# Value product of attention: one block of four units per batch in place of two blocks of two

## The reference

```
q = rope(proj(layernorm(x), Wq, bq)) * Dh ** -0.5      # 16 heads of 16
k = rope(proj(ctx, Wk, bk));  v = proj(ctx, Wv, bv)
scores = einsum('bhqd,bhkd->bhqk', q, k)               # causal mask
probs  = softmax(scores)
out    = einsum('bhqk,bhkd->bhqd', probs, v)           # the value product
x      = x + tanh(g) * (out @ Wo.T + bo)
...                                                    # router, top 2 of 32 experts, capacity 140 per expert
```

## Time and profile before

| | us |
|---|---|
| median of 3 runs | 768.54 |
| lowest and highest run | 766.45, 773.82 |
| span of the profiled execution | 763.2 |
| TensorE (PE) busy | 669.2 (88%) |
| VectorE (DVE) busy | 525.3 (69%) |
| ScalarE (ACT) busy | 403.5 (53%) |
| GpSimd (POOL) busy | 323.1 (42%) |
| value product L1665 busy | 62.0 |

### The profile page before, as it was taken

The page is one execution under the profiler, slowest core; times in us unless marked ns, Lnnn a source line. Parts: engine busy times, 40 slices in busy tenths (PEclk is TensorE's granted clock), DMA queues, the critical chain, the costliest instruction groups (busy, mean ns, idle before and its releaser), DMA issues.

```text
span 763.2 us, 17579 instructions
## 1 busy us (share of the span) xinstructions
PE 669.2 (88%) x5275; PEld 530.8 (70%) x5275; DVE 525.3 (69%) x1548; ACT 403.5 (53%) x1569; POOL 323.1 (42%) x340
## 2 busy tenths in 40 slices
PE   8799999999999999999987313699999999999992
PEld 4466666666666666666655201499999999999992
DVE  6665786767867678676899888677778644445441
ACT  2367778877788777888684566022222222222220
POOL 3443362443624436243112000435566565665643
PEclk9899999999999999999999655799999999999996
DMA  5600010210102001010001601168888998888921
GB/s 182 221 32 25 26 51 24 74 27 25 50 23 73 26 25 50 23 49 1 26 26 49 242 0 16 44 195 229 263 259 249 266 269 255 269 235 267 276 42 15
DMA packets 57852, 85.83 MB, mean 112 GB/s; under 512 B 11452, under 2 KB 28468, under 8 KB 57652
## 3 DMA queue, kind: packets, MB, share of 16 engines
q1 hardware_dynamic: 47588, 74.37, 29.7%
q0 software_dynamic: 9216, 9.76, 7.8%
q10 hardware_dynamic: 976, 0.89, 0.4%
HBM read 72.30 MB, written 12.69 MB: 111 GB/s over the span
## 4 chain that ended last, share of the span: by engine, by line
PE 49%; ACT 19%; DVE 18%; issue 8%; DMA 2%; POOL 2%; ACTq 1%; DVEq 1%; POOLq 0%
PE pair L1005 19%; PE bank L1015 10%; ACT arena L1311 8%; DVE arena L1484 5%; PE pair L1637 4%; PE bank L1600 3%; ACT arena L574 2%; PE pair L1646 2%; PE bank L1665 2%; ACT arena L1260 2%; PE bank L1027 2%; PE pair L1632 2%; ACT arena L1299 1%; DMA arena<-rows,slot_row 1%; DVE we L1465 1%
## 5 line engine op out<-in xcount | busy, mean ns | idle before, releaser
L1311 ACT ACTIVATE arena<-pair,arena 112x112 f32<-112x112 f32 x512 | 175.5, 365 | 67.0 <-DVE arena L1484 62.2
L1005 PE MATMUL pair<-arena,we 128*128 128x140 f32 x1024 | 137.9, 283 | 0.7 <-issue 0.6
L896 POOL DMA_INDIRECT rows_out<-arena,slot_row x64 | 94.4, 1475 | 94.6 <-DVE arena L949 81.4
L1005 PEld LDWEIGHTS pair<-arena,we 128*128 128x128 f32 x1024 | 128.5, 190 | 1.2 <-issue 1.2
L926 ACT ACTIVATE arena<-pair 128x140 f32<-128x140 f32 x160 | 45.8, 287 | 149.6 <-PE pair L1005 103.0
L961 DVE SCALAR_TENSOR_TENSOR arena<-arena,pair 128x140 f32<-128x140 f32 x160 | 47.6, 297 | 95.5 <-ACT arena L926 50.4
L1311 ACT ACTIVATION_READ_ACCUMULATOR arena<-pair,arena 112x1 f32 x512 | 109.8, 214 | 0.0
L885 POOL DMA_INDIRECT arena<-rows,slot_row x64 | 63.1, 986 | 83.8 <-issue 83.8
L1015 PE MATMUL bank<-arena,we 128*128 128x140 f32 x512 | 83.7, 286 | 0.0
L1484 DVE TENSOR_REDUCE arena<-pair 112x8 f32<-112x896 f32 x64 | 68.9, 1077 | 17.4 <-PE pair L1637 16.8
L1646 PEld LDWEIGHTS pair<-tab,arena 112*112 112x112 f32 x512 | 51.5, 133 | 30.3 <-issue 28.3
(11 more groups left out here) (209 smaller groups left out, 1195.2 us busy)
## 6 DMA issues: line engine op xcount, KB each, us to landing
we<-w_experts_in SPq DMA_DIRECT2D x192, 256.0 KB
wa<-w_adapters_in SPq DMA_DIRECT2D x16, 384.0 KB
arena<-ctx_in SPq DMA_DIRECT2D x8, 448.0 KB, 4.4
arena<-x_in SPq DMA_DIRECT2D x8, 448.0 KB, 4.0
rows_out<-arena SPq DMA_DIRECT2D x8, 448.0 KB, 3.3
rows<-arena SPq DMA_DIRECT2D x8, 448.0 KB, 3.3
arena<-ways_in SPq DMA_DIRECT2D x1, 1024.0 KB, 5.2
arena<-rows,slot_row POOLq DMA_INDIRECT x64
```

Source lines behind the costliest of these rows:

```text
L896: nc.gpsimd.indirect_dma_start(d["out"], bass.IndirectOffsetOnAxis(ap=slot_row[:, h, e:e + 1], axis=0), yr[e % 2][:, h, :], None, compute_ ...
L1005: last = nc.tensor.matmul(banks[m % 4][:, part * CAP:(part + 1) * CAP], w[:, col0:col0 + 128], xet[j % 2][:, c, :], start=(c == 0), stop=( ...
L1311: last = nc.scalar.activation(pr[s % 2][:, j, :], banks[BS[s % 4]][0:T, j * T:(j + 1) * T], ACT.Exp, bias=nmx[s // 2 % 2][:, s % 2, j:j + ...
```

## The change

The value product of a batch is issued in one call. `WEIGH` goes from 5 to 7 and the call is made for every fourth unit, at steps 7, 11, 15 and 3. It loops over the four units inside the loop over heads, so that four matmuls in a row go to the four column tiles. It waits for the evictions of all four units, and counts one per batch on `s_pv` in place of two. The turned probabilities of two batches are kept: `prt` has eight buffers, four of them in the arena as before, four in the part of `we[1][1]` behind `pcos`. The waits on `s_pv` of the evictions and of the value and attention reads are put in the new count.

```diff
-TURN, WEIGH, DENOM, SUMS, ATT = 2, 5, 6, 7, 8
+TURN, WEIGH, DENOM, SUMS, ATT = 2, 7, 6, 7, 8
+KEPT_UNITS = 2 * NU
...
-    prt = [take(T, [HU, T]) for _ in range(4)]
...
+    prt_at = [2 * NT + i * HU * T for i in range(NU)]
+    prt = [we[1][1][0:T, at:at + HU * T].rearrange("p (a b) -> p a b", a=HU) for at in prt_at]
+    prt += [take(T, [HU, T]) for _ in range(NU)]
...
                     if u % 2 == 1:
                         wait(act, s_ptr, GU * (g - back) + u + 1)
-                        wait(act, s_pv, GU // 2 * (g - back) + u // 2 - 1)
-                        nc.scalar.copy(prt[u % 4].rearrange("p a b -> p (a b)"),
+                        wait(act, s_pv, GB * (g - back) + u // NU - 1)
+                        nc.scalar.copy(prt[u % KEPT_UNITS].rearrange("p a b -> p (a b)"),
... (the same on VectorE for even units)
-            wait(dve, s_pv, GU // 2 * (q - 1))
+            wait(dve, s_pv, GB * (q - 1))
...
-                        wait(dve, s_pv, GU // 2 * (g - back) + (u + NU) // 2)
+                        wait(dve, s_pv, GB * (g - back) + u // NU + 1)
...
-        def weigh(q, par, u):
-            b, k = u // NU, u % NU
-            if u == 0:
+        def weigh(q, par, b):
+            if b == 0:
                 wait(pe, s_v, 2 * (q + 1))
-            if k == 0:
-                wait(pe, s_att, GB * q + b)
+            wait(pe, s_att, GB * q + b)
             for i in range(2):
-                wait(pe, s_pte[i], GU // 2 * q + u // 2 + 1)
+                wait(pe, s_pte[i], GU // 2 * q + NU // 2 * (b + 1))
             for j in range(HU):
-                for i in range(2):
-                    h = head_of(k + i, j)
-                    rows = slice(32 * (k + i), 32 * (k + i) + 32)
+                for k in range(NU):
+                    h = head_of(k, j)
+                    rows = slice(32 * k, 32 * k + 32)
                     last = nc.tensor.matmul(
                         banks[BO][rows, j // 2 * T:(j // 2 + 1) * T],
                         vx[par][:, b * (NH // 2) + h // 2, 2 * (j % 2):2 * (j % 2) + 2, :].rearrange("p a d -> p (a d)"),
-                        prt[(u + i) % 4][:, j, :], start=(j % 2 == 0), stop=(j % 2 == 1))
+                        prt[(b * NU + k) % KEPT_UNITS][:, j, :], start=(j % 2 == 0), stop=(j % 2 == 1))
...
                 for back, u in unit_at(s, WEIGH, own, prev):
-                    if u % 2 == 0:
-                        weigh(g - back, (par + back) % 2, u)
+                    if u % NU == 0:
+                        weigh(g - back, (par + back) % 2, u // NU)
```

More of the change, by code:

```diff
@@ L389, in program @@
     warm = we[1][0][0:T, 0:NT // 2]
+    prt_at = [2 * NT + i * HU * T for i in range(NU)]
+    prt = [we[1][1][0:T, at:at + HU * T].rearrange("p (a b) -> p a b", a=HU) for at in prt_at]
+    prt += [take(T, [HU, T]) for _ in range(NU)]
+    assert len(prt) == KEPT_UNITS
     size = we[1][0][0:T, 3 * NT:3 * NT + GB * C].rearrange("p (b c) -> p b c", b=GB)
@@ L468, in program @@
                    (s_rope, 4), (s_kz, GB), (s_v, 2), (s_s, GU), (s_mx, GU // 2), (s_exp, GU), (s_ptr, GU),
-                   (s_pte[0], GU // 2), (s_pte[1], GU // 2), (s_pv, GU // 2), (s_att, GB),
+                   (s_pte[0], GU // 2), (s_pte[1], GU // 2), (s_pv, GB), (s_att, GB),
                    (s_rden, GB), (s_rdx, GB), (s_rt, GB), (s_rdent, GB), (s_x1, GB), (s_ln2, 1), (s_ln2a, 1), (s_mean, 1), (s_size, 1), (s_zc, 1), (s_rs2, 1), (s_mv3, 1), (s_st, 1),
@@ L1488, in group @@
                         wait(dve, s_ptr, GU * (g - back) + u + 1)
-                        wait(dve, s_pv, GU // 2 * (g - back) + u // 2 - 1)
-                        nc.vector.tensor_copy(prt[u % 4].rearrange("p a b -> p (a b)"),
+                        wait(dve, s_pv, GB * (g - back) + u // NU - 1)
+                        nc.vector.tensor_copy(prt[u % KEPT_UNITS].rearrange("p a b -> p (a b)"),
                                               banks[BS[u % 4]][0:T, 0:HU * T]).then_inc(s_pte[0], 1)
```

## The result

| | before | after |
|---|---|---|
| median of 20 runs, us | 767.40 | 772.04 |
| lowest and highest | 764.52, 773.82 | 767.29, 776.23 |
| span of the profiled execution | 763.2 | 772.1 |
| mean granted clock in it | 0.948 | 0.923 |

The ratio is 1.0058, 95% interval 1.0038 to 1.0079: 0.6% slower, inside the range that was given and on the side of the central forecast, but 4.6 us where 1.1 were reckoned. The cause is the one cost that the prediction set at nothing, the clock. Lines after the change stand about four lower in the code: L1667 is the value product, L1636 the mask, L1641 the scores, L1303 ScalarE's eviction.

The account below looks back on a forecast made before the run. The eviction loop was taken to pace five of eight pairs, TensorE alone only step 11. The median 768.5 plus 1.1 us gave 769.6, stated as 769.5; own range 766 to 773.5, stretched to 764 to 777.5 for 8 in 10.

Parts of the forecast that it names:

- What bounds the stage: Attention stage: five of eight pairs paced by the loop scores, maximum, exponentials, eviction, next scores; only step 11 by TensorE alone.
- The first view: Busy time by stretches: TensorE busy 18.89 of 20 us at clock 1.00, which alone would make TensorE the bound.
- the 3.6 forecast: Mask's wait for the eviction, behind steps 5, 9, 13 and 1: to grow by roughly 3.6 us per trip.
- The 0.23 at 236.75: Gap before ScalarE's eviction, taken as its own turnaround, which stays; if wrong, 1.6 us in all come back.
- The block: Value product of a batch, 32 records at 0.028 us between starts: 1.06 us, where a batch had 1.80.
- the +0.16 of step 11: Longer block at step 11 with no wait over it: 0.16 us per trip, +1.1 us in seven trips.
- the third and fourth tile: Rival: in the value product they bring nothing, distance 0.047, block 1.65 us; +7.7 us, 776.2 us; chance 10%.
- loads of four tiles in one row group: Rival: value product's loads are not hidden, block 1.77 us; +9.4 us, 778 us; chance 5%.
- No fall, 0.: Clock term: TensorE at 17.6 busy of 20 us keeps its full clock, so the cost is 0.
- The stretch that I leaned on: Stretch from 400 us, TensorE 15.92 busy at clock 1.00, taken as evidence that the clock would not fall.
- a term of +1.1: The sum's only term: step 11 in seven trips, 7 x 0.16 = +1.1 us.
- TensorE was not the bound: Rival that TensorE is the bound after all: all 23.7 us come back, 745 us, -3.1%; chance 8%.

## Why the prediction was right, and where it was not

**What bounds the stage** was read rightly. The first view alone (94% busy) would have given 745 us. The excess of the mask's two matmuls over 0.55 us told that five of eight pairs wait for the eviction; after the change those distances stood: steps 4 to 6 took 5.06 us in both, 6 to 8 5.72 in both. 28 us of TensorE's own work went out of the stage, and of it only the 0.09 us per trip behind step 8 came back. The waits of the mask grew by 0.5, 1.0, 0.9 and 1.0 to 1.35 us per trip behind steps 5, 9, 13 and 1; 0.9 each was forecast, so behind step 5 the growth was half of that, and in all it was 3.4 to 3.8 for the 3.6 forecast. The eviction of step 9 against the scores before it, after:

```profile
245.50 0.53 ACT L1303 COPY arena<-pair 112x448 f32<-112x448 f32 x1 [0.23 <-ACT arena L1264]
```
and before:
```profile
237.66 1.01 PE L1637 MATMUL pair<-arena 32*112 32x224 f32 x8
...
242.75 0.53 ACT L1299 COPY arena<-pair 112x448 f32<-112x448 f32 x1 [0.23 <-ACT arena L1260]
```

It is 5.09 us behind the scores before, 5.01 after (scores at 240.49): 0.08 us sooner, which is the small gain of steps 8 to 10, where none was forecast. The 0.23 at 236.75 in the earlier trace rows was ScalarE's turnaround, as I took it: behind a copy that has just ended it is there after the change too, in step 9 as shown and in step 7 (239.58).

**The block** was mis-sized, on the side of caution: I took 0.028 us between records from a quarter of a full-array load; (0.98 - 0.26) / 31 is 0.023, the lower bound, half of what two tiles gave, and the block is 0.91 and not 1.06. So the +0.16 of step 11, the only term of my sum, is +0.02. The 0.023 is a mean: in the trace the records of the four tiles start 7 ns apart, and the eight rounds of a block begin within 0.705 us, just as the eight rounds of two did (0.704). So the third and fourth tile ride along for nothing, and loads of four tiles in one row group are hidden as completely as of two. By the Trainium skill ("TensorE: Matmul & The Clock Gate", section "The mechanism") a load overlaps matmuls in flight only if its row group differs. The trace does not agree for column tiles, 0.023 us a record as above; the same section also has loads into a background weight buffer pulled ahead, and the trace does not speak against that. The Trainium skill's section "Measured speedup vs the span model" on the same page lets a packed group last as long as one matmul, plus about 4 ns for each further tile. The trace agrees in kind, with 7 ns.

**The failed step is the clock: "No fall, 0."** I compared busy shares over 20 us, 17.6 to come against 15.92 held at full clock. The mean that I reckoned was right (16.5 to 18.7 in the trips, 17.7 on average from 60 to 360 us), and the inference was wrong. The stretch that I leaned on was no proof either: it ends at 420 us, and in that same execution the clock went to half at 423.9. The term costs what the sum lacked: 8.2 us in the profiled execution, 4.6 in the medians. Ahead of each of the six falls the trace shows the same: TensorE waits 1.03 to 1.58 us for the eviction in one of the steps 1, 5 or 9, and 0.8 to 2.2 us after the end of that wait the clock is at half. A fall makes the steps behind it slow, and where one of them is paced by TensorE (steps 2, 3, 10, 11 and the last trip) the time is lost for good; elsewhere the waits absorb part of it.

That the total came out in the range and on the forecast's side is partly luck: a term of +1.1 that was not there, and one of +4.6 that I had at nothing. The rivals are settled. TensorE was not the bound. The third and fourth tile do bring something. And a rival that I had not listed, the clock, is what happened.

**Open:** which of the many equal waits is followed by a fall. In the changed kernel the mask waited 1 us or more 21 times between 40 us and the last scores, and six falls came; the 20 executions of it spread from a span of 765.5 us at mean clock 0.936 to 774.4 at 0.919, with the same instructions. In the kernel before, waits of 1.05 and 1.00 us in the last trip and one of 1.19 in the first had no fall behind them, nor had one of 1.30 in the last trip with the gaps filled. So a wait of that length came before every fall here, and most such waits had none.

## What to carry to other kernels

Before counting on freed time of an engine, take the distance of its instructions at the point where a stage turns over and subtract what they take when nothing is waited for; if that excess is there, the engine is not the bound, whatever its busy share. Where TensorE is not the bound, work taken from it is not free either: it can lose its clock, and then lose time in the steps where it is the bound. Move other work into the gap, or fill it with an idle matmul of few instructions, and measure both; filling alone gave back the loss here and no more. Look at the waits step by step to judge the risk for the clock: the mean over a long stretch hid it here.

## What the runs showed of the hardware

- Leaving out half of the value product made the kernel 0.67% slower (0.40 to 0.95), and in the profiled execution all of the 9.2 us that its stage took longer lie at stretches of half clock.
- The clock fell to 1.2 GHz in the middle of a stage in which TensorE was otherwise at work all the time, behind waits of 1.03 to 1.58 us: six times in one execution, 31 us in all.
- Records of 32-bit matmuls of 112 columns on four column tiles start every 0.023 us on average (four of them 7 ns apart, then the next four), on two tiles in turn every 0.047 in a block of 16 and 0.036 in a block of 32.
- A loop body longer by 16 records a batch brought stalls of 2.64 and 2.82 us at the two jumps back, and 18 fetches of 16 KB of instructions between 167 and 371 us, where the shorter body had none.
